# A cross attention whose probabilities are turned by VectorE and four DMAs instead of by TensorE

## The reference

```
def _L1_xattn_ref(x_q, x_k, x_v, mask, W_q, b_q, W_k, b_k, W_v, b_v, W_o, b_o):
    Q = _split_heads(x_q @ W_q.T + b_q)
    K = _split_heads(x_k @ W_k.T + b_k)
    V = _split_heads(x_v @ W_v.T + b_v)
    scores = jnp.einsum('bhqd,bhkd->bhqk', Q, K) / jnp.sqrt(jnp.float32(D_K))
    scores = jnp.where(mask == 0, jnp.float32(-1000000000.0), scores)
    attn = jax.nn.softmax(scores, axis=-1)
    out = jnp.einsum('bhqk,bhkd->bhqd', attn, V)
    out = out.transpose(0, 2, 1, 3).reshape(...)
    return out @ W_o.T + b_o

x = x + _L1_xattn_ref(_layernorm(x), ctx_1024, ctx_1024, mask_Bx1x1xS2_if1, ...)
```

## Time and profile before

| what | value |
|---|---|
| median of the runs | 2270.99 us |
| the profiled execution: span from first to last instruction | 2270.1 us |
| TensorE (PE) busy | 1957.3 us, 86% of the span |
| VectorE (DVE) busy | 1626.0 us, 72% |
| ScalarE (ACT) busy | 1640.6 us, 72% |
| GpSimd (POOL) busy | 899.0 us, 40% |
| core's DMA traffic | 93.89 MB, mean 41 GB/s |

### The profile page before, as it was taken

The page is one execution under the profiler, slowest core; times in us unless marked ns, Lnnn a source line. Parts: engine busy times, 40 slices in busy tenths (PEclk is TensorE's granted clock), DMA queues, the critical chain, the costliest instruction groups (busy, mean ns, idle before and its releaser), DMA issues. The chain is left out here.

```text
span 2270.1 us, 55792 instructions
## 1 busy us (share of the span) xinstructions
PE 1957.3 (86%) x15563; PEld 1549.6 (68%) x15563; DVE 1626.0 (72%) x5153; ACT 1640.6 (72%) x4441; POOL 899.0 (40%) x1338
## 2 busy tenths in 40 slices
PE   3799999999999999995350579999999989858997
PEld 3688888888888888883240257777777756526775
DVE  5677777777777777764778758888888878854564
ACT  3588888888888888876486368888888878735553
POOL 1533443444433333422245123333333357533554
PEclk8699999999999999997585789999999999969999
DMA  4211111111110111100000022222222100013222
GB/s 134 73 34 34 33 33 33 33 33 33 29 28 27 30 33 33 33 4 1 0 0 0 0 73 66 74 65 65 74 65 65 52 2 0 1 28 84 89 83 84
DMA packets 124106, 93.89 MB, mean 41 GB/s; under 512 B 14417, under 2 KB 101937, under 8 KB 123905
## 3 DMA queue, kind: packets, MB, share of 16 engines
q1 hardware_dynamic: 122550, 90.88, 14.6%
q10 hardware_dynamic: 1194, 1.58, 0.2%
q0 software_dynamic: 288, 0.56, 0.1%
HBM read 88.26 MB, written 4.72 MB: 41 GB/s over the span
## 5 line engine op out<-in xcount | busy, mean ns | idle before, releaser
L750 ACT ACTIVATE a_prob<-a_neg,a_nmax 128x289 f32<-128x289 f32 x512 | 270.5, 530 | 79.0 <-DVE a_nmax L679 72.9
L1686 ACT ACTIVATE b_prob<-b_neg,b_nmax 128x257 f32<-128x257 f32 x512 | 255.2, 500 | 71.2 <-DVE b_nmax L1633 71.1
L645 POOL TENSOR_TENSOR a_xn<-a_z,g 128x256 f32<-128x256 f32 x128 | 93.3, 729 | 526.3 <-DVE a_z L705 526.3
L807 PE MATMUL a_score<-a_xnT,a_qT 128*128 128x290 f32 x1536 | 274.8, 315 | 1.1 <-DVE a_qT L726 1.1
L835 PE MATMUL a_out<-a_probT,a_xn 128*128 128x256 f32 x1024 | 263.6, 380 | 0.3 <-DVE a_probT L690 0.3
L679 DVE CUSTOM_DVE_ANT_0 a_neg<-a_score,a_bias 128x289 f32<-128x289 f32 x512 | 222.0, 459 | 46.4 <-PE a_score L807 40.0
L807 PEld LDWEIGHTS a_score<-a_xnT,a_qT 128*128 128x128 f32 x1536 | 216.5, 191 | 43.8 <-issue 43.2
L1633 DVE CUSTOM_DVE_ANT_0 b_neg<-b_score,b_bias 128x257 f32<-128x257 f32 x512 | 195.9, 421 | 50.8 <-PE b_score L1729 48.6
L755 ACT ACTIVATE a_prob<-a_prob,a_rinv 128x256 f32<-128x256 f32 x512 | 230.4, 499 | 1.1 <-DVE a_rinv L717 1.0
L835 PEld LDWEIGHTS a_out<-a_probT,a_xn 128*128 128x128 f32 x1024 | 175.0, 191 | 13.6 <-DVE a_probT L690 0.6
L1607 POOL TENSOR_TENSOR b_last_part<-b_v_rows,b_prob 128x128 f32<-128x128 f32 x128 | 52.0, 406 | 318.2 <-ACT b_prob L1686 318.2
(11 more groups left out here) (479 smaller groups left out, 5192.2 us busy)
## 6 DMA issues: line engine op xcount, KB each, us to landing
a_raw<-in_ctx SPq DMA_DIRECT2D x128, 128.0 KB, 3.4
b_raw<-in_ctx SPq DMA_DIRECT2D x128, 128.0 KB, 3.3
m_wide<-expert_weights SPq DMA_DIRECT2D x128, 128.0 KB, 2.9
a_kept<-keep SPq DMA_DIRECT2D x32, 257.0 KB, 3.9
b_kept<-keep SPq DMA_DIRECT2D x32, 257.0 KB, 3.5
b_v_rows<-ctx_tail_values SPq DMA_DIRECT2D x32, 256.0 KB, 3.6
a_tail<-latents_normalised SPq DMA_DIRECT2D x64, 64.0 KB
latents_normalised<-lat_affine SPq DMA_DIRECT2D x8, 256.0 KB, 2.3
```

Of the source, the lines that this page charges most:

```text
L750: nc.scalar.activation(prob[:, par, grp, :], neg[:, grp, :], ACT.Exp, bias=nmax[:, par, grp:grp + 1], scale=-1.0, accum_out=rsum[:, par, g ...
L807: last = nc.tensor.matmul(score_ps[grp % 2][:, 0:even(KEYS0)], qT[:, a, un, bn, 4 * grp:4 * grp + 4, :], xnT[:, c, n, :], start=(p == 0), ...
L1686: nc.scalar.activation(prob[:, n, grp, :], neg[:, par, grp, :], ACT.Exp, bias=nmax[:, par, grp:grp + 1], scale=-1.0, accum_out=rsum[:, n, ...
```

## The change

TensorE no longer transposes the probabilities, and the two copies out of PSUM go. In place of them VectorE turns the probabilities of batch s+1 in blocks of 32 by 32 (`turn_blocks`), in two instructions, one per 128 keys, from `prob` to a new tile `blocks`. A block takes every fourth key. In `blocks` the partition is 32 times the row group plus the key's index in its block. Four DMAs from SyncE's queue (`spread_prob`), one per group of 32 partitions, then carry the blocks to the partitions of the keys in `probT`, 1 KB per row. The value products of batch s wait for these DMAs of the step before. `blocks` and `probT` have two slots. The keys and values of s+3 get PSUM banks of their own names (`k_ps`, `v_ps`), and waits that kept them apart from the transposes are gone.

```diff
-        probT = sb("b_probT", [P, 2, CH])
+        blocks, probT = sb("b_blocks", [P, 2, 4, 2, GROUPS, L]), sb("b_probT", [P, 2, 4, 2, GROUPS, L])
...
-        turn_ps = [psum("b_turn0"), psum("b_turn1")]
+        k_ps, v_ps = psum("b_k"), psum("b_v_ps")
...
+                def spread_prob(g, j):
+                    s, n = g * 8 + j, (j + 1) % 2
+                    sp.wait_ge(blocks_ready, s + 2)
+                    wait(sp, out_ready, s)
+                    for i in range(4):
+                        sp.dma_start(probT[:, n, i].rearrange("p t g l -> p (t g l)"),
+                                     blocks[i * L:(i + 1) * L, n].rearrange("c r t g l -> c r (t g l)")).then_inc(probT_loaded[n], 16)
...
                         wait(sp, in_turned, s + 1)
                         load_raw(g + 1, j)
+                    if live(g, j, 1):
+                        spread_prob(g, j)
...
+                def turn_blocks(g, j):
+                    s, n = g * 8 + j, (j + 1) % 2
+                    dve.wait_ge(exped, s * 4 + 8)
+                    wait(dve, out_ready, s)
+                    for kt in range(2):
+                        last = nc.vector.transpose(blocks[:, n, :, kt].rearrange("p r g l -> p g r l"),
+                                                   prob[:, (j + 1) % 4, :, kt * P:(kt + 1) * P].rearrange("p g (c r) -> p g r c", r=4))
+                    last.then_inc(blocks_ready, 1)
...
-                    if live(g, j, 0):
-                        dve.wait_ge(turned[0], s + 1)
-                        nc.vector.tensor_copy(probT[:, 0, :], turn_ps[0][:]).then_inc(probT_ready[0], 1)
+                    if live(g, j, 1):
+                        turn_blocks(g, j)
...
-                    if live(g, j, 0):
-                        act.wait_ge(turned[1], s + 1)
-                        nc.scalar.activation(probT[:, 1, :], turn_ps[1][:], ACT.Copy).then_inc(probT_ready[1], 1)
...
-                def turn(g, j, kt):
-                    for grp in range(GROUPS):
-                        last = nc.tensor.transpose(turn_ps[kt][:, grp * P:(grp + 1) * P],
-                                                   prob[:, j % 4, grp, kt * P:(kt + 1) * P], k.ident[:])
-                    last.then_inc(turned[kt], 1)
-
                 def values(g, j, kt):
-                    s = g * 8 + j
-                    pe.wait_ge(probT_ready[kt], s + 1)
+                    if kt == 0:
+                        pe.wait_ge(probT_loaded[j % 2], (g * 4 + (j // 2 + 1)) * 64)
...
-                    if here:
-                        pe.wait_ge(exped, s * 4 + 4)
-                        pe.wait_ge(k_ready, upto(g, s, 3))
-                        turn(g, j, 0)
-                        pe.wait_ge(v_ready, upto(g, s, 3))
-                        turn(g, j, 1)
```

More of the change, by code:

```diff
@@ L1537, in xattn1 @@
         scored, masked, exped, rinv_ready = (sem(f"b_{n}") for n in ("scored", "masked", "exped", "rinv_ready"))
-        turned, probT_ready = [sem(f"b_turned{n}") for n in range(2)], [sem(f"b_probT_ready{n}") for n in range(2)]
+        blocks_ready, probT_loaded = sem("b_blocks_ready"), [sem(f"b_probT_loaded{u}") for u in range(2)]
         out_ready, weight_ready, last_ready, own_ready, sum_ready, oT_ready, proj_ready, x_added = (
@@ L1546, in tile_of @@
             return g * 2 + (j + ahead) // 4
-        def upto(g, s, n):
-            return min(s + n, B) if isinstance(g, int) else s + n
         with nc.Block() as block:
@@ L1664, in step @@
                         dve.wait_ge(kept_loaded[(j + 3) // 4 % 2], (g + (j + 3) // 8 + 1) * 16)
-                        nc.vector.scalar_tensor_tensor(kT[:, n, :], turn_ps[0][:, 0:N_CTX], k.bk1, kept[:, (j + 3) // 4 % 2, n, :],
+                        nc.vector.scalar_tensor_tensor(kT[:, n, :], k_ps[:, 0:N_CTX], k.bk1, kept[:, (j + 3) // 4 % 2, n, :],
                                                        ALU.add, ALU.mult).then_inc(k_ready, 1)
@@ L1706, in step @@
                         act.wait_ge(v_done, s + 4)
-                        nc.scalar.activation(v[:, (j + 3) % 8], turn_ps[1][:, 0:2 * P].rearrange("p (t d) -> p t d", d=D), ACT.Copy)\
+                        nc.scalar.activation(v[:, (j + 3) % 8], v_ps[:, 0:2 * P].rearrange("p (t d) -> p t d", d=D), ACT.Copy)\
                             .then_inc(v_ready, 1)
@@ L1730, in score @@
                     last.then_inc(scored, 1)
-                def turn(g, j, kt):
-                    for grp in range(GROUPS):
-                        last = nc.tensor.transpose(turn_ps[kt][:, grp * P:(grp + 1) * P],
-                                                   prob[:, j % 4, grp, kt * P:(kt + 1) * P], k.ident[:])
-                    last.then_inc(turned[kt], 1)
                 def values(g, j, kt):
-                    s = g * 8 + j
-                    pe.wait_ge(probT_ready[kt], s + 1)
+                    if kt == 0:
+                        pe.wait_ge(probT_loaded[j % 2], (g * 4 + (j // 2 + 1)) * 64)
                     for grp in range(GROUPS):
                         rows = slice(grp * 32, grp * 32 + 32)
-                        last = nc.tensor.matmul(out_ps[rows, 0:P], v[:, j, kt, rows], probT[:, kt, grp * P:(grp + 1) * P],
+                        last = nc.tensor.matmul(out_ps[rows, 0:P], v[:, j, kt, rows], probT[:, j % 2, :, kt, grp, :],
                                                 start=False, stop=(kt == 1), skip_group_check=True)
@@ L1773, in step @@
                             pe.wait_ge(keys_ready, tile_of(g, j, 3) + 1)
-                        if here:
-                            pe.wait_ge(probT_ready[0], s + 1)
                         wait(pe, k_ready, s + 3)
-                        nc.tensor.matmul(turn_ps[0][:, 0:N_CTX], k.wk1[:], turned_in[:, n, C0:C0 + N_CTX], start=True, stop=True).then_inc(k_done, 1)
-                        if here:
-                            pe.wait_ge(probT_ready[1], s + 1)
+                        nc.tensor.matmul(k_ps[:, 0:N_CTX], k.wk1[:], turned_in[:, n, C0:C0 + N_CTX], start=True, stop=True).then_inc(k_done, 1)
                         wait(pe, v_ready, s + 3)
                         for kt in range(2):
-                            last = nc.tensor.matmul(turn_ps[1][:, kt * D:(kt + 1) * D], turned_in[:, n, C0 + kt * P:C0 + (kt + 1) * P], k.wv1[:],
+                            last = nc.tensor.matmul(v_ps[:, kt * D:(kt + 1) * D], turned_in[:, n, C0 + kt * P:C0 + (kt + 1) * P], k.wv1[:],
                                                     start=True, stop=True)
```

## The result

The changed kernel took 2463.23 us (median of 4 runs, 2462.27 to 2465.17) against 2271.55 for the kernel before, measured beside it: 1.0842 times as long, 95% interval 1.0826 to 1.0857. The prediction was 2467 us.

The account below looks back on a forecast made before the run. TensorE was taken to bound the stage before, a loop between VectorE and ScalarE after: 1.51 us more a batch times 127 is 191.8, plus 3.8 at the end, on 2271.0 gives about 2467 us; range 2372 to 2530 us.

Parts of the forecast that it names:

- The loop: VectorE and ScalarE: turns, reciprocal, next masks, exponentials, next turns follow one another; period 2t + 3.44 us, t per turn.
- The price of a turn: VectorE's block turn of 512 values per partition, four apart, was taken at 0.96 us, like the reduction of `b_own`.
- rival A: VectorE's turns cost as much as adjacent values, 0.61 us each: period 4.66 us, 2377 us in all; chance 0.28.
- Reciprocal to first mask: On VectorE, from the reciprocal's start to the first mask: a mean of 0.59 us over four batches.
- First mask to turns: From VectorE's first mask until it can go on behind ScalarE's last exponential: 2.85 us.
- The period: Time per batch in the changed stage: 2 x 0.96 + 3.44 = 5.36 us, 1.51 more than 3.85.
- The end: Last batch, uncovered: 7.37 us from its exponentials to its `b_own` instead of 3.56, so 3.8 us more.
- DMAs hidden: The four new DMAs a batch take 4.7 us from turns to last landing, within 7.7 us of cover.
- Rival C: The DMAs become the bound, landing at 9.4 us: period 6.19 us, 2577 us in all; chance 0.08.
- TensorE's clock: In the changed stage TensorE, busy 2.92 of 5.36 us, was expected to stay at clock 1.00, 2.4 GHz.
- rival B: TensorE's clock falls; if all its work doubled, 5.84 us a batch would bound the stage, 2528 us; chance 0.10.
- TensorE's gain: Eight transposes a batch go, 0.93 us less for TensorE, worth nothing since it waits.

Follow-up runs that it names:

- experiment 8: Changed kernel plus eight transposes of the identity a batch on TensorE, which nobody reads: 2468.46 us, 1.0864 of the kernel before.
- moved version: Changed kernel with turns and reciprocal moved behind the first two masks of the next batch: 2446.04 us, 1.0758 of the kernel before.
- experiment 7: The half version with each group's scores waiting only for their own mask, and each mask for its own scores: 2298.07 us, 1.0110 of the kernel before.
- half version: Changed kernel, but VectorE turns only the first 128 keys, TensorE the rest; adjacent reads, reciprocal and turn behind two masks: 2304.78 us, 1.0144 of the kernel before.

## Why the prediction was right, point by point

- **The loop.** Shown. VectorE and ScalarE wait for each other in all 94 batches. When one term, the turns, got 0.77 us shorter, the kernel got 98 us faster; three quarters of the DMAs were worth 2.9 us, and a higher clock, with more work for TensorE, nothing. No run shortened ScalarE's side alone; that the exponentials belong to the loop is read from the waits.
- **The price of a turn.** Taken 0.96 us from the reduction's row, measured 1.00 from start to start (1080 ns each). With adjacent reads it is 1.23 / 2 = 0.62 (690 ns), the value of rival A. So the read order tells forecast and rival apart: both values were in the rows of before, each at its own kind of read the earlier trace rows. The Trainium skill's rule that a new 16-byte line at each access costs extra (Advanced Engine Details and Errata, SBUF Cachelines) agrees with this; only steps of four and of one were run, so that the line is the reason is not shown. The other rule of the Trainium skill (Vector Engine (DVE) Microarchitecture Reference, The reshape front-end and per-opcode configuration) is not contradicted: the adjacent turn takes as long as a copy of as many values, 690 against 692 ns.
- **Reciprocal to first mask.** 0.59 us predicted. Measured 0.05 in two batches of four, 1601.13 - 1600.13 = 1.00 and 1611.69 - 1610.83 = 0.86 in the others, mean 0.49. Behind a turn the reciprocal has 138 ns, and its follower starts 0.05 us after it, not 0.16 as in the earlier trace rows; why is not shown.
- **First mask to turns.** 2.85 predicted, 2.81 and 1603.97 - 1601.13 = 2.84 measured.
- **The period.** 5.36 predicted. The first and last reciprocal of the 128:

```profile
1341.02 0.14 DVE L1662 RECIPROCAL b_rinv<-b_rsum 128x4 f32<-128x4 f32 x1
...
2013.69 2.05 DVE L1650 STREAM_TRANSPOSE b_blocks<-b_prob 128x512 f32<-128x512 f32 x2 [0.99 <-ACT b_prob L1702]
2015.66 0.14 DVE L1662 RECIPROCAL b_rinv<-b_rsum 128x4 f32<-128x4 f32 x1
...
2021.54 0.29 DVE L1691 TENSOR_TENSOR b_own<-b_out,b_turned_in 128x128 f32<-128x128 f32 x1 [3.64 <-PE b_out L1750]
```

  (2015.66 - 1341.02) / 127 = 5.31 us. The turns were 0.08 dearer, the way to the mask 0.10 and the way from mask to turns 0.03 cheaper than thought, which is the whole difference: 2.00 + 0.49 + 2.82 = 5.31. Over the stage, from the first turns to the last, it is (2013.69 - 1339.02) - 489.0 = 185.7 us more than before where 191.8 stood.
- **The end.** 7.37 us from the last exponentials to `b_own` were predicted, 2021.54 - 2013.69 = 7.85 passed, 4.3 us more than before instead of 3.8. The DMAs took what was forecast: the turns were over at about 2015.7, and the value products could start 4.7 us later:

```profile
2020.39 1.08 PE L1750 MATMUL b_out<-b_probT,b_v 128*32 128x128 f32 x16 [1.97 <-DMA b_probT<-b_blocks]
```

  The term that was too small is the last one, from there to `b_own`: 2021.54 - 2020.39 = 1.15 us instead of 0.75. Before, it had been 1829.05 - 1828.21 = 0.84, so 0.31 of it is new. The clock was 0.50 in 2019 to 2022 us, and it was 1.00 at this place before (1827.0 to 1829.1 us). So there a low clock lay on the path, once.
- **What the sum left to luck.** The first turns start at 1339.02, where the first reciprocal stood at 1336.49 before, 2.5 us later. This delay is older than the changed stage. Its first DMA, before and after:

```profile
1323.72 0.34 SPq L1561 DMA_DIRECT2D b_kept<-keep  x1
```

```profile
1326.27 0.34 SPq L1557 DMA_DIRECT2D b_kept<-keep  x1
```

  The last DMA ahead of the stage starts anywhere from 1320.45 to 1324.26 us in the profiled executions of the fourteen kernels, so this looks like the difference from one execution to the next, and is no term of the change. 2.5 + 185.7 + 4.3 (the end) = 192.5 us, against 193.3 between the spans; 0.8 fall behind the stage. The stage itself grew by 190.0 us where 195.6 were forecast. That the total came out within 4 us is in part luck.
- **DMAs hidden.** Right, with both parts slightly off and in opposite directions: issues 0.63 us instead of 0.5, landing 2.7 instead of 3.2, so 3 x 0.63 + 2.7 = 4.6 us to the last landing against 4.7. Rival C is out.
- **TensorE's clock.** The step that was wrong, with next to no effect. I expected 1.00. The stretch had a mean of 0.82, while TensorE was busy 368 of 500 us, and this mean is a mixture of the two levels, 1.2 and 2.4 GHz:

```profile
1408.00:1412.00 4.00, 1.93 (x28) 1.12 (x28) 3.39 (x13) 2.21 (x9) 0.40 (x1) 1.00 0.74 175
...
1444.00:1448.00 4.00, 4.00 (x30) 2.81 (x26) 3.99 (x13) 1.86 (x7) 2.15 (x5) 0.50 0.34 79
```

  So rival B's mechanism was at work in part. The key product, for one, took 538 ns in the mean instead of 432:

```profile
L1776 PE MATMUL b_k<-b_turned_in,wk1T 128*128 128x257 f32 x188 | 84.3, 538 | 0.0
```

  TensorE's busy time was 367.88 / 94 = 3.91 us a batch, not the 2.92 forecast. It could not set the time, because 132 us of idle time were left even so and VectorE waited for TensorE only 1.0 us; experiment 8 agrees.
- **TensorE's gain.** Worth nothing, as forecast: it waits for masks instead. It is not even visible in TensorE's busy time, 3.91 us a batch against 3.86 before.

What stays open is, first, that the moved version is held by the way from last mask to next scores is read from its trace and not tested: experiment 7 made that wait shorter in the half version only, where TensorE was nearly full. Second, the half version was not tried with the key order made elsewhere than in TensorE's read.

## What to carry to other kernels

In this kernel a gap in a queue that work of an older batch filled was not spare time: when that work was replaced by work on the newest batch, the gap and the work both entered the period. Look for the small wait (2.6 us in 10 batches here) that says how near two engines are to waiting for each other, and add up the loop rather than the engines' busy time. Reading with a step cost more on VectorE and on TensorE alike here, so moving the step to the other engine helped only while that engine idled.

## What the hardware showed that I had not expected

- VectorE's block turn of 128 x 512 fp32 values took 1080 ns reading four values apart and 690 ns reading 32 adjacent ones.
- TensorE's product of a fixed 128 x 128 operand with fp32 columns that lie four apart took 441 ns for 128 and 664 for 256 at clock 1.00, against 282 for 129 and 432 for 257 adjacent ones.
- The granted clock had a mean of 0.82 with TensorE busy 74% of the time and its idle time in pieces under 2 us, and went to and fro between 0.50 and 1.00 within a few batches; before, a stretch with 5.93 of 10 us busy had 1.00, and in experiment 8, busy 77%, the mean was 0.96.
- A DMA of 128 KB from SBUF to SBUF landed after 2.7 us, no later than one from HBM (2.9), and with the queue at 61.7% of 16 engines, against 25.7% before, the landing of the HBM loads did not get longer.
